# Two 64-row TensorE matmuls in opposite halves of the array, in the modulated-convolution kernel's Q2 and W units

## The reference

```python
def _layer(x, style, w, b, mw, mb, typ):
    s = style @ mw.T + mb
    weight = SCALE * w * s[:, None, :, None]
    demod = lax.rsqrt(jnp.sum(weight * weight, axis=(2, 3)) + EPS)
    weight = weight * demod[:, :, None, None]
    # 'same':       conv of 3 taps
    # 'upsample':   transposed conv of stride 2, then blur with 2 * [1,3,3,1]/8
    # 'downsample': blur with [1,3,3,1]/8, then conv of stride 2
out = x
for i, typ in enumerate(('same', 'upsample', 'same', 'downsample')):
    out = _layer(out, style, weights[i], biases[i], mod_w[i], mod_b[i], typ)
return x + out
```

## Time and profile before

| | |
|---|---|
| median of 3 executions | 679.83 us (677.91 to 680.50) |
| profiled execution, its own time | 678.67 us |
| its span, first to last instruction | 676.8 us |
| TensorE busy with matmuls | 665.0 us, 98% of the span, 4502 matmuls |
| weight loads busy | 620.3 us, 92% |
| VectorE, ScalarE, GpSimd busy | 468.0, 312.1, 366.7 us |
| granted TensorE clock, mean | 1.000 |

### The profile page before, as it was taken

How to read it: one execution, slowest core, us unless ns; L and a number is a source line. 1 busy time by engine, 2 the same in 40 slices (tenths; PEclk the granted TensorE clock), 3 DMA queues, 4 the chain that set the end, 5 groups by cost and what they waited for, 6 DMA issues and landing times.

```text
span 676.8 us, 12255 instructions
## 1 busy us (share of the span) xinstructions
PE 665.0 (98%) x4502; PEld 620.3 (92%) x4502; DVE 468.0 (69%) x702; ACT 312.1 (46%) x494; POOL 366.7 (54%) x387
## 2 busy tenths in 40 slices
PE   8998999999999999999999999999999999999987
PEld 7887999999999999999999999999999999999986
DVE  5896778675766696766766876767567867576551
ACT  4335444544554444454453454454454444455441
POOL 2446555556556556556555575555655655665410
PEclk9999999999999999999999999999999999999999
DMA  7238775758777558786666787666877576877763
GB/s 257 58 92 211 180 167 144 186 168 211 181 191 160 156 159 207 181 201 157 161 180 175 179 198 172 155 181 171 210 183 177 140 190 161 205 188 196 157 151 135
DMA packets 130603, 117.33 MB, mean 173 GB/s; under 512 B 6064, under 2 KB 97136, under 8 KB 130544
## 3 DMA queue, kind: packets, MB, share of 16 engines
q1 hardware_dynamic: 130176, 116.30, 68.4%
q10 hardware_dynamic: 368, 0.25, 0.1%
HBM read 36.57 MB, written 33.82 MB: 104 GB/s over the span
## 4 chain that ended last, share of the span: by engine, by line
PE 94%; DVE 3%; issue 1%; ACT 1%; POOL 0%; DVEq 0%; ACTq 0%; POOLq 0%
PE po L174 17%; PE po L175 16%; PE po L176 16%; PE pg L174 8%; PE pg L176 8%; PE pg L175 8%; PE pg L179 4%; PE pg L180 4%; PE pm L176 3%; PE pm L174 3%; PE pm L175 3%; PE pe L398 1%; PE pg L407 1%; PE pe L391 1%; PE pe L401 0%
## 5 line engine op out<-in xcount | busy, mean ns | idle before, releaser
L174 PE MATMUL po<-xh,W 128*128 128x256 f32 (+1 forms) x640 | 217.8, 340 | 3.5 <-DVE T L741 1.8
L175 PE MATMUL po<-xl,W 128*128 128x256 f32 (+1 forms) x640 | 217.0, 339 | 0.0
L176 PE MATMUL po<-xh,W 128*128 128x256 f32 (+1 forms) x640 | 216.7, 339 | 0.0
L174 PEld LDWEIGHTS po<-xh,W 128*128 128x128 f32 x640 | 125.1, 195 | 13.8 <-issue 4.2
L176 PEld LDWEIGHTS po<-xh,W 128*128 128x128 f32 x640 | 125.6, 196 | 12.3
L175 PEld LDWEIGHTS po<-xl,W 128*128 128x128 f32 x640 | 125.6, 196 | 9.9
L666 POOL TENSOR_TENSOR Q2l<-Q2f,Q2h 128x512 fp32r<-128x512 f32 x30 | 71.6, 2387 | 81.9 <-ACT Q2h L551 81.9
L741 DVE SCALAR_TENSOR_TENSOR T<-po,DD,M 128x512 f32<-128x512 f32 x64 | 48.0, 751 | 78.3 <-PE po L176 47.2
L512 ACT CAST xh<-X 128x1032 fp32r<-128x1032 f32 x64 | 81.0, 1266 | 37.8 <-PE po L176 36.8
L732 DVE TENSOR_TENSOR xl<-X,xh 128x1032 fp32r<-128x1032 f32 x64 | 96.4, 1506 | 2.9 <-ACT xh L512 2.9
L561 ACT CAST W<-Wf 128x512 fp32r<-128x512 f32 x64 | 46.7, 729 | 100.9 <-DVE Wf L773 66.2
(11 more groups left out here) (176 smaller groups left out, 1526.7 us busy)
## 6 DMA issues: line engine op xcount, KB each, us to landing
X<-in_xin SPq DMA_DIRECT2D x64, 516.0 KB, 4.3
out<-T SPq DMA_DIRECT2D x64, 512.0 KB, 3.6
W<-W SPq DMA_DIRECT2D x93, 256.0 KB, 4.3
W<-W SPq DMA_DIRECT2D x31, 384.0 KB, 5.6
V<-V SPq DMA_DIRECT2D x32, 128.0 KB, 5.1
V<-W SPq DMA_DIRECT2D x32, 64.0 KB, 3.6
V<-Vx SPq DMA_DIRECT2D x32, 64.0 KB, 3.2
E<-in_ed SPq DMA_DIRECT2D x1, 768.0 KB, 7.3
```

Of the source, the lines that this page charges most:

```text
L174: eng.matmul(o, wh_, rh, start=first, stop=False)
L175: eng.matmul(o, wh_, rl, start=False, stop=False)
L176: return eng.matmul(o, wl_, rh, start=False, stop=last)
```

## The change

The products of 64 rows are made in pairs, units 0 and 1 together, and units 5 and 6 together. The moving tile now has the high part in both halves (`Q3h[:, :, 1]`, `Gh[:, :, 3]`), and a new weight tile (`A2m`, `Cm`) has the high weights in its lower rows and the low weights in its upper rows: one matmul of 128 rows gives two of the three products (`a_both`, `c_both`), where there were two. The third product, high weights by the low part, is a matmul of 64 rows; that of unit 0 (5) is done in the lower rows of the array and that of unit 1 (6) in the upper rows, one right after the other and into two PSUM banks (`a_half`, `c_half`). So a pair has four matmuls as before, of which two have 64 rows.

Around them: unit 1 (6) is issued inside unit 0 (5), and its bank is waited for (`other`, `free`) before the pair's last matmuls; unit 0's semaphore increment sits on the third matmul of the four. The low parts get full tiles: GpSimd subtracts once with 512 elements a partition where it subtracted 256 in 128 partitions and 256 in 64. In the prologue ScalarE, VectorE and GpSimd each fill half of the new weight tiles, and the low tiles `A2l` and `Cl` are halved.

```diff
-        Gl = sb("Gl", [128, 2, 3, 128], F32R)
+        Gl = sb("Gl", [128, 2, 4, 128], F32R)
-        Q3l = sb("Q3l", [128, 2, 128], F32R)
+        Q3l = sb("Q3l", [128, 2, 2, 128], F32R)
+        A2m = sb("A2m", [128, 256], F32R)
+        Cm = sb("Cm", [128, 2, 128], F32R)
...
+            def other(g, u):
+                n = PLACE[g, u]
+                free(n)
+                return bank(pg[n % NP], 1)[:, :, 0]
...
-                    return lone_mm(pe, o, *w, Q3h[:, :, 1], first, last)
+                def a_both(o, d, first):
+                    pe.matmul(o, A2m[:, 128 * d:128 * d + 128], Q3h[:, :, 1], start=first, stop=False)
+                def a_half(o, d, p):
+                    return pe.matmul(o, A2h[p, 256 + 128 * d:384 + 128 * d], Q3l[p, :, 1], start=False, stop=True)
...
-                    return lone_mm(pe, o, Ch[:, 2 + d, :], Cl[:, 2 + d, :], Gh[:, :, 3], first, last)
+                def c_both(o, d, first):
+                    pe.matmul(o, Cm[:, d], Gh[:, :, 3], start=first, stop=False)
+                def c_half(o, d, p):
+                    return pe.matmul(o, Ch[p, 2 + d], Gl[p, :, 3], start=False, stop=True)
...
-                    m = a_(o[1], 1, 0, False, True)
-                elif u == 1:
-                    m = a_(o[0], 1, 1, True, True)
+                    a_both(o[1], 0, False)
+                    m1 = other(g, 1)
+                    a_both(m1, 1, True)
+                    a_half(o[1], 0, lo).then_inc(s_c, 1)
+                    m = a_half(m1, 1, hi)
...
-                    m = c_(o[1], 3, 3, False, True)
-                else:
-                    m = c_(o[0], 4, 3, True, True)
+                    c_both(o[1], 0, False)
+                    m1 = other(g, 6)
+                    c_both(m1, 1, True)
+                    c_half(o[1], 0, lo).then_inc(s_c, 1)
+                    m = c_half(m1, 1, hi)
...
-            pe.wait_ge(s_cl, 1)
+            pe.wait_ge(s_cl, 2)
...
-            act.copy(A2h[:], A2f[:]).then_inc(s_k0, 1)
+            act.copy(A2h[:], A2f[:])
+            act.copy(A2m[lo], A2f[lo, 256:512]).then_inc(s_k0, 1)
...
-            act.copy(Ch[:], Cf[:]).then_inc(s_k0, 1)
+            act.copy(Ch[:], Cf[:])
+            act.copy(Cm[lo], Cf[lo, 2:4]).then_inc(s_k0, 1)
...
-                pool.tensor_tensor(Q3l[:], Q3f[:, :, 0], r32(Q3h[:, :, 0]), ALU.subtract).then_inc(s_q3l, 1)
-                pool.wait_ge(s_q3l, 2 * g + 1)
-                lone_low(pool, Q3h[hi, :, 1], Q3f[hi, :, 1]).then_inc(s_q3l, 1)
-                pool.wait_ge(s_q3l, 2 * g + 2)
+                pool.tensor_tensor(Q3l[:], Q3f[:], r32(Q3h[:]), ALU.subtract).then_inc(s_q3l, 1)
+                pool.wait_ge(s_q3l, g + 1)
...
-                    pool.tensor_tensor(Gl[:, :, 2], Gf[:, :, 2], r32(Gh[:, :, 2]), ALU.subtract).then_inc(s_gl, 1)
-                    pool.wait_ge(s_gl, 3 * g + 2)
-                    lone_low(pool, Gh[hi, :, 3], Gf[hi, :, 3]).then_inc(s_gl, 1)
+                    pool.tensor_tensor(Gl[:, :, 2:4], Gf[:, :, 2:4], r32(Gh[:, :, 2:4]), ALU.subtract).then_inc(s_gl, 1)
...
-            tt(A2l[:], A2f[:], r32(A2h[:]), ALU.subtract).then_inc(s_a2, 1)
+            tt(A2l[:], A2f[:, 0:256], r32(A2h[:, 0:256]), ALU.subtract)
+            tt(A2m[hi], A2f[hi, 256:512], r32(A2h[hi, 256:512]), ALU.subtract).then_inc(s_a2, 1)
```

More of the change, by code:

```diff
@@ L77, in build @@
         Q3h = sb("Q3h", [128, 2, 2, 128], F32R)
-        Q3l = sb("Q3l", [128, 2, 128], F32R)
+        Q3l = sb("Q3l", [128, 2, 2, 128], F32R)
         ID = sb("ID", [128, 2, 128])
         A2h = sb("A2h", [128, 512], F32R)
-        A2l = sb("A2l", [128, 512], F32R)
+        A2l = sb("A2l", [128, 256], F32R)
+        A2m = sb("A2m", [128, 256], F32R)
+        Cm = sb("Cm", [128, 2, 128], F32R)
         B1h = sb("B1h", [128, 6, 2, C], F32R)
@@ L86, in build @@
         Ch = sb("Ch", [128, 4, 128], F32R)
-        Cl = sb("Cl", [128, 4, 128], F32R)
+        Cl = sb("Cl", [128, 2, 128], F32R)
         q3s = sb("q3s", [128, 2, C])
@@ L319, in conv, with free, unit, a_ @@
                 part(po[b % 2][:, 256:512], (1, 3), 2 * HW).then_inc(s_o, 1)
-            def unit(g, u):
-                n = PLACE[g, u]
-                o = [bank(pg[n % NP], 1)[:, :, 0]] if u in (1, 6) else [bank(pg[n % NP], 2)[:, :, v] for v in range(2)]
+            def free(n):
                 if n >= NP:
                     pe.wait_ge(s_ce, n - NP + 1)
[L327 to L330, removed]
-                    return lone_mm(pe, o, *w, Q3h[:, :, 1], first, last)
+            def other(g, u):
+                n = PLACE[g, u]
+                free(n)
+                return bank(pg[n % NP], 1)[:, :, 0]
+            def unit(g, u):
+                if u in (1, 6):
+                    return
+                n = PLACE[g, u]
+                o = [bank(pg[n % NP], 2)[:, :, v] for v in range(2)]
+                free(n)
+                def a_(o, d, first, last):
+                    w = [t[:, 128 * d:128 * d + 128] for t in (A2h, A2l)]
+                    return split_mm(pe, o, *w, Q3h[:, :, 0], Q3l[:, :, 0], first, last)
+                def a_both(o, d, first):
+                    pe.matmul(o, A2m[:, 128 * d:128 * d + 128], Q3h[:, :, 1], start=first, stop=False)
+                def a_half(o, d, p):
+                    return pe.matmul(o, A2h[p, 256 + 128 * d:384 + 128 * d], Q3l[p, :, 1], start=False, stop=True)
                 def b_(o, v, p, first, last):
@@ L341, in c_ @@
                     d = v - p
-                    if p < 3:
-                        return split_mm(pe, o, Ch[:, d, :], Cl[:, d, :], Gh[:, :, p], Gl[:, :, p], first, last)
-                    return lone_mm(pe, o, Ch[:, 2 + d, :], Cl[:, 2 + d, :], Gh[:, :, 3], first, last)
+                    return split_mm(pe, o, Ch[:, d, :], Cl[:, d, :], Gh[:, :, p], Gl[:, :, p], first, last)
+                def c_both(o, d, first):
+                    pe.matmul(o, Cm[:, d], Gh[:, :, 3], start=first, stop=False)
+                def c_half(o, d, p):
+                    return pe.matmul(o, Ch[p, 2 + d], Gl[p, :, 3], start=False, stop=True)
                 if u == 0:
                     pe.wait_ge(s_q3h, g + 1)
-                    pe.wait_ge(s_q3l, 2 * g + 2)
-                    a_(o[0], 0, 0, True, True)
-                    a_(o[1], 0, 1, True, False)
-                    m = a_(o[1], 1, 0, False, True)
-                elif u == 1:
-                    m = a_(o[0], 1, 1, True, True)
+                    pe.wait_ge(s_q3l, g + 1)
+                    a_(o[0], 0, True, True)
+                    a_(o[1], 1, True, False)
+                    a_both(o[1], 0, False)
[3 more added lines that the diff above has]
+                    m = a_half(m1, 1, hi)
                 elif u == 2:
@@ L370, in unit @@
                     pe.wait_ge(s_gh, 2 * g + 1)
-                    pe.wait_ge(s_gl, 3 * g + 1)
+                    pe.wait_ge(s_gl, 2 * g + 1)
                     c_(o[0], 0, 0, True, True)
@@ L376, in unit @@
                     pe.wait_ge(s_gh, 2 * g + 2)
-                    pe.wait_ge(s_gl, 3 * g + 3)
+                    pe.wait_ge(s_gl, 2 * g + 2)
                     c_(o[0], 2, 1, True, False)
@@ L650, in q3_full @@
                     pool.wait_ge(s_q3h, g)
-                    pool.wait_ge(s_q3l, 2 * g)
+                    pool.wait_ge(s_q3l, g)
                 for a in range(2):
@@ L676, in low @@
                     pool.wait_ge(s_gh, 2 * g + 2)
-                    pool.tensor_tensor(Gl[:, :, 2], Gf[:, :, 2], r32(Gh[:, :, 2]), ALU.subtract).then_inc(s_gl, 1)
-                    pool.wait_ge(s_gl, 3 * g + 2)
-                    lone_low(pool, Gh[hi, :, 3], Gf[hi, :, 3]).then_inc(s_gl, 1)
-                    pool.wait_ge(s_gl, 3 * g + 3)
+                    pool.tensor_tensor(Gl[:, :, 2:4], Gf[:, :, 2:4], r32(Gh[:, :, 2:4]), ALU.subtract).then_inc(s_gl, 1)
+                    pool.wait_ge(s_gl, 2 * g + 2)
             def identity(g):
@@ L689, in _ @@
             pool.wait_ge(s_b1, 1)
-            pool.tensor_tensor(Cl[:], Cf[:], r32(Ch[:]), ALU.subtract).then_inc(s_cl, 1)
+            pool.tensor_tensor(Cl[:], Cf[:, 0:2], r32(Ch[:, 0:2]), ALU.subtract).then_inc(s_cl, 1)
+            pool.wait_ge(s_cl, 1)
+            pool.tensor_tensor(Cm[hi], Cf[hi, 2:4], r32(Ch[hi, 2:4]), ALU.subtract).then_inc(s_cl, 1)
+            pool.wait_ge(s_cl, 2)
             pool.wait_ge(s_sc, SC_D)
@@ L761, in full @@
                         dve.wait_ge(s_gh, 2 * g - 3 + u)
-                        dve.wait_ge(s_gl, 3 * g - 2 if u == 2 else 3 * g)
+                        dve.wait_ge(s_gl, 2 * g - 3 + u)
                     m = tt(cols(Gf[:, :, 2 * u - 4:2 * u - 2]), cols(bank(src, 2)), bc2(gs(D10c, g), 2), ALU.mult)
@@ L785, in g_low @@
                 dve.wait_ge(s_gh, 2 * g + 2)
-                tt(Gl[:, :, 2], Gf[:, :, 2], r32(Gh[:, :, 2]), ALU.subtract).then_inc(s_gl, 1)
-                lone_low(dve, Gh[hi, :, 3], Gf[hi, :, 3]).then_inc(s_gl, 1)
```

(7 more changed lines are left out.)

## The result

The changed kernel took 698.53 us (median of 4, 696.16 to 699.89) beside 680.0 us of the kernel before: ratio 1.0275, 95% interval 1.0239 to 1.031. A second set of runs gave 695.95 us beside 678.98: ratio 1.0256, 1.023 to 1.0281. It is slower, by 17.0 to 18.5 us.

What follows compares the result with a forecast made beforehand. The prediction took TensorE, never without work from sample to sample, as the bound. 62 pairs x 0.315 us = 19.5 us, added to the median of 679.83, gave 699.3 us, range 689 to 706, chance 0.83.

Steps and rivals of the forecast that it cites:

- What bounds the kernel: In the loop TensorE is never without work, so whatever is added to its stream counts once in full.
- The two steps: Per pair, going from 128 to 64 rows and back drains TensorE: 0.18 to 0.19 us and 0.20 us.
- The prologue's rows: Trace rows of the kernel before, at 14.14 and 39.05 us, from which both row-count changes were priced.
- The size of a pair: Loss per pair: 0.26 us with halves side by side, 0.37 with loads in turn; the middle, 0.315, taken.
- X: Start of a pair's second 128-row matmul; next work was to start at X + 0.62 or 0.73, before X + 0.36.
- The number of pairs: 32 groups by two is 64; the prologue's first and last pair add no loss, so 62 pay.
- The rest at nothing: GpSimd's larger subtractions, later increments, bank waits and prologue copies cost nothing; prologue 0, give or take 0.3 us.
- the cover: Slack between the end of GpSimd's `Gl` subtraction and unit 5's start: 5.4 us against up to 0.9 us more.
- A: Rival: 64-row tiles between 128-row ones need no drain; 62 x 0.12 = 7.4 us gained, 672.4 us; chance 0.08.
- B: Rival: no drain, but the halves share the load path and don't overlap; no change, 679.8 us; chance 0.04.
- C: Rival: going from lower to upper rows drains too; 0.58 us a pair, 36 us, 715.8 us; chance 0.05.

Runs made afterwards that it cites:

- filled run: Kernel before with 14 extra matmuls of 256 columns (results unused) at sample 124, in TensorE's wait for the last group's mirrored weights: 679.05 us, ratio 1.0002.
- the lower rows' experiment: Changed kernel with the second half of each pair in the lower rows too, so both 64-row matmuls use the same rows: 704.98 us, ratio 1.0376.

## Why the prediction was right

What bounds the kernel: shown. TensorE's stream was lengthened by 16.7 us in the stretch without waits, and the time rose by 17.0 to 18.5.

The two steps: shown. Both have the form of the earlier trace rows: the load 0.21 us after the start of the last matmul, the matmul after it listed 0.10 longer. With the row count put back nearly all of the loss goes (0.2 us of 16.7 between the marks), with the steps doubled it grows from 0.29 to 0.79 a pair. The prologue's rows carried over to fp32r matmuls in the loop, in both directions, and the cost is nearly the same with f32 on one side of the step and with fp32r on both. That is also how the Trainium skill has it ("TensorEngine Tiling (Array Packing)", Key Properties): changing the mode drains, changing the tile doesn't. Both halves of the rule agree now, the second with loads of both rows that start together.

The size of a pair: the term that was too large. I took 0.315, the middle between halves fully side by side (0.26) and loads in turn (0.37). The loads go side by side, and a pair costs 0.288: with that the sum is 62 x 0.288 = 17.9 us in place of 19.5. It is 0.03 above the 0.26 of that end. 0.02 of it stands in the rows: the conv's load starts at X + 0.53 and not 0.52, and its first matmul really starts 0.11 after its load and not 0.10.

The number of pairs: 62 is too high as a count of what is seen. The 58 behind the last early wait pay in full, 16.7 us; what the others cost is mostly absorbed by waits, of which the forecast left out the two at 54.5 and 60.6 us.

So that 699.3 came as near as 0.8 us to the first median is in part luck: the pairs gave 2.8 us less than forecast, and the end of the kernel added 2.9 in that profile. Against the second set of runs the forecast of +19.5 was 2.5 us too high.

The rest at nothing: right as far as it can be seen. GpSimd's `Q3l` takes 1.37 us and its second `Gl` 1.29, less than the 1.55 and 1.47 that two pieces took:

```profile
306.78 1.29 POOL L704 TENSOR_TENSOR Gl<-Gf,Gh 128x512 fp32r<-128x512 f32 x1
319.93 1.37 POOL L687 TENSOR_TENSOR Q3l<-Q3f,Q3h 128x512 fp32r<-128x512 f32 x1 [4.44 <-ACT Q3h L570]
```

`Gl` is done at 308.07. Its unit 5 starts at 314.06, so the cover has even grown (6.0 us instead of 5.4). The prologue came out 0.26 us earlier (39.59 against 39.85), but this tells little: the kernel before itself is there at 39.13 in its filled run, whose edit comes only at the end. Whether the copies cost 0.3 us or nothing isn't shown.

The rivals. A (no drain, 672.4) is refuted; its half that is true, two halves for the time of one, is worth 0.12 us a pair and is inside the 0.29. B (halves don't overlap) is refuted by the lower rows' experiment, 704.98 against 698.53. C (a drain between the halves, 715.8) is refuted by loads that start together.

## What to carry to other kernels

Matmuls of 64 rows side by side do run two for the time of one, but the block that they form pays on entering and on leaving: here about 0.20 us each, over three distances of a 256-column matmul for both. Count what a block saves before counting what a matmul saves. This one saves 0.12 and pays 0.40; each of this kernel's 64-row products would add 0.06 to the saving (1.5 distances instead of 2), so that it would take seven in one block to come out even, by this estimate, and the order of the units gives two. Before building such a change, look in the trace for any place where the row count changes already: a prologue with a few small matmuls showed the price to within 0.02 us a step.

## What the runs showed of the hardware that I had not expected

Weight loads into different row halves start together (within one load's 0.19 us), also in a steady stream, where the double halves keep 0.12 us; loads into the same half start 0.10 us apart. I had left this open.

A step costs in two parts, a load held back by about 0.09 us and a matmul that waits about 0.10 us for it, and the price is nearly the same in both directions, with f32 on one side or fp32r on both: 0.18 to 0.20 us in the earlier trace rows, 0.20 in the loop.

After the wait of 1.8 to 3.0 us near the end, some executions ran a stretch of TensorE at 1.2 GHz: starts 0.43 us apart (679.27, 679.70) instead of 0.23. Filling the wait kept the clock near 1.000 (0.997 to 1.000) but gained no time in either kernel.
